# A decoder's three cross attentions: the order of work ahead of the first scores

## The reference

```python
x = x + _L1_xattn_ref(_layernorm(x), ctx_1024, ctx_1024, Wq, bq, Wk, bk, Wv, bv, Wo, bo)
# inside:
q = heads(layernorm(x) @ Wq + bq)          # 32 x 16 x 56 x 8
k = heads(ctx @ Wk + bk)                   # 32 x 16 x 1500 x 8
v = heads(ctx @ Wv + bv)
out = softmax(q @ k.T * scale) @ v         # per sequence and head
return merge(out) @ Wo + bo
```

## Time and profile before

| | |
|---|---|
| median of 3 runs | 3799.75 us (3795.43 to 3820.61) |
| profiled execution, its own time | 3812.16 us |
| its span in the trace | 3810.4 us |
| PE busy | 3447.9 us (90%) |
| DVE busy | 2381.6 us (63%) |
| ACT busy | 2087.9 us (55%) |
| POOL busy | 1618.1 us (42%) |
| mean granted share of PE's clock | 0.948 |

### The profile page before, as it was taken

How to read it: one execution, slowest core, us unless ns; L and a number is a source line. 1 busy time by engine, 2 the same in 40 slices (tenths; PEclk the granted TensorE clock), 3 DMA queues, 4 the chain that set the end, 5 groups by cost and what they waited for, 6 DMA issues and landing times. The chain is left out here.

```text
span 3810.4 us, 110666 instructions
## 1 busy us (share of the span) xinstructions
PE 3447.9 (90%) x46768; PEld 2411.7 (63%) x46768; DVE 2381.6 (63%) x4435; ACT 2087.9 (55%) x3581; POOL 1618.1 (42%) x1884
## 2 busy tenths in 40 slices
PE   7986669999999697889999999799999999999878
PEld 5654237777777344657777777343446777777548
DVE  5523568877776354468877776233667877777552
ACT  4333557777777222147777776334446777776511
POOL 1100157677674000047777664000336776776121
PEclk9999979999999798899999999899999999999967
DMA  4054136665664243036666564110015666656423
GB/s 164 2 227 168 47 84 155 153 159 144 154 156 97 51 117 82 4 88 152 149 160 148 149 158 100 47 61 23 13 43 140 156 154 152 159 145 153 123 68 106
DMA packets 206109, 439.22 MB, mean 115 GB/s; under 512 B 88210, under 2 KB 101111, under 8 KB 205448
## 3 DMA queue, kind: packets, MB, share of 16 engines
q1 hardware_dynamic: 202760, 430.07, 42.7%
q0 software_dynamic: 1440, 1.83, 0.2%
q10 hardware_dynamic: 1440, 0.52, 0.1%
HBM read 184.67 MB, written 5.40 MB: 50 GB/s over the span
## 5 line engine op out<-in xcount | busy, mean ns | idle before, releaser
L1562 DVE TENSOR_REDUCE x_bank_top<-ps 112x1 f32<-112x500 f32 x2304 | 1414.2, 672 | 447.8 <-PE ps L1264 440.8
L1410 ACT ACTIVATE x_probs_t<-ps 128x896 f32<-128x896 f32 x768 | 703.3, 916 | 127.6 <-PE ps L1285 122.6
L1264 PE MATMUL ps<-x_keys,x_queries 96*112 96x500 bf16 x2304 | 653.6, 382 | 42.5 <-DMA x_queries<-x_query_part 18.6
L1285 PEld LDWEIGHTS ps<-x_queries,x_keys 128*128 128x128 bf16 x9216 | 509.2, 97 | 245.6 <-issue 139.8
L1285 PE MATMUL ps<-x_queries,x_keys 128*128 128x112 bf16 x9216 | 580.9, 213 | 5.4 <-ACT x_probs_t L1410 4.2
L1299 PE MATMUL ps<-x_probs_t,x_values 128*32 128x112 f32 x18432 | 483.4, 261 | 8.9 <-ACT x_probs_t L1412 8.9
L1299 PEld LDWEIGHTS ps<-x_probs_t,x_values 128*32 128x32 f32 x18432 | 436.9, 110 | 70.1 <-issue 39.4
L1488 POOL TENSOR_TENSOR x_key_part<-x_key_whole,x_nothing 128x500 bf16<-128x500 f32 x270 | 337.3, 1249 | 256.8 <-ACT x_key_whole L1394 256.8
L1412 ACT ACTIVATE x_probs_t<-ps 128x448 f32<-128x448 f32 x768 | 414.5, 540 | 0.0
L1264 PEld LDWEIGHTS ps<-x_keys,x_queries 96*112 96x112 bf16 x2304 | 262.6, 131 | 170.9 <-DVE x_bank_top L1562 69.8
L1496 POOL TENSOR_TENSOR x_key_part<-x_key_left,x_nothing 128x500 bf16<-128x500 f32 x270 | 335.8, 1244 | 14.1
(11 more groups left out here) (510 smaller groups left out, 4332.1 us busy)
## 6 DMA issues: line engine op xcount, KB each, us to landing
x_keys<-x_key_part SPq DMA_DIRECT2D x1152, 192.0 KB, 3.8
x_ctx_t<-in_ctx_t SPq DMA_DIRECT2D x96, 750.0 KB, 6.2
cm_ctx_n<-in_ctx_n SPq DMA_DIRECT2D x32, 768.0 KB, 6.2
cm_ctx_t<-in_ctx_t SPq DMA_DIRECT2D x32, 750.0 KB, 8.6
x_queries<-x_query_part SPq DMA_DIRECT2D x558, 28.0 KB, 2.5
e_share<-m_weight_rows SPq DMA_DIRECT2D x32, 448.0 KB, 6.0
m_w<-in_L_ffn_experts SPq DMA_DIRECT2D x16, 768.0 KB, 5.7
e_share<-m_weight_rows SPq DMA_DIRECT2D x8, 896.0 KB, 5.3
```

Of the source, the lines that this page charges most:

```text
L1264: nc.tensor.matmul(ps[0:RW, n, 0:KB], queries[i // 2 % 2][0:TALL, p, i % 2, :], keys[i % 2][0:TALL, p, KB * n:KB * n + KB], start=True, st ...
L1285: mm = nc.tensor.matmul(ps[:, turned_bank(i, p) + c // VC, RW * (c % VC):RW * (c % VC) + RW], keys[i % 2][:, p, KT * c:KT * c + KT], queri ...
L1410: nc.scalar.activation(goal[:, 0:VR - 1], ps[:, bank:bank + VR - 1, 0:VC * RW], ACT.Exp, scale=scale).then_inc(exp_done, 1)
L1562: nc.vector.tensor_reduce(bank_top[0:RW, p, n:n + 1], ps[0:RW, n, 0:KB], AX_X, ALU.max).then_inc(topped, 1)
```

## The change

The same instructions are issued, three times as before, with other banks, in another order and with other waits:

- Norm takes the banks of the centred tokens as a list. Chunks 0 to 3 lie in banks 0, 3, 4, 5 and their means of squares in banks 1, 2, 1, 2. All pieces of the keys but the second go through bank 6.
- PE projects the three pieces of the keys of sequence 0 and the first chunk of the queries before it goes on with the norm of chunks 1 to 3. The last three pieces of the keys stand between the projections of the queries.
- ACT finishes chunk 0 of the norm, keeps and splits its queries and issues three slots of half 0; only then it takes the logarithm of chunk 1 and goes on. Its slots of half 1 come behind all that.
- SP waits for the high parts, issues three key slots, then slots of queries and keys by and by as their parts come.
- The scores of sequence 0 wait for the first kept chunk of the queries and the last logarithm instead of all four chunks; `scores_by_key` waits for all four.

```diff
-LEAD_BANKS = (6, 7, 6, 4, 5, 6)
+LEAD_BANKS = (6, 7, 6, 6, 6, 6)
+TOKEN_BANKS = (0, 3, 4, 5)
...
-        norm = Norm(chip, x, xn, True, scratch[:CH], scratch[CH:], (4, 5, 4, 5))
+        norm = Norm(chip, x, xn, True, scratch[:CH], scratch[CH:], (1, 2, 1, 2), None, TOKEN_BANKS)
...
             sp.wait_ge(zeros_ready, 2 * PARTS)
+            sp.wait_ge(lead_high, NB_)
+            for s in (0, 1, 2):
+                key_slots(sp, 0, 0, s)
+            sp.wait_ge(q_mid, 2)
+            query_slots(sp, 0, 0, 1)
+            query_slots(sp, 0, 0, 4)
+            sp.wait_ge(lead_mid, NB_)
+            key_slots(sp, 0, 0, 3)
+            key_slots(sp, 0, 0, 4)
+            sp.wait_ge(q_low, 2)
+            query_slots(sp, 0, 0, 2)
             sp.wait_ge(lead_low, NB_)
-            for s in range(SLOTS):
-                key_slots(sp, 0, 0, s)
-            sp.wait_ge(q_low, 2)
-            for h in range(2):
-                for s in range(SLOTS // 2):
-                    query_slots(sp, 0, h, s)
+            key_slots(sp, 0, 0, 5)
+            for s in (1, 4, 2):
+                query_slots(sp, 0, 1, s)
             stack_keys(0, 1)
...
                 if i == 0 and p == 0:
-                    pe.wait_ge(q_kept, CH)
+                    pe.wait_ge(q_kept, 1)
+                    norm.wait_log(pe, CH - 1)
...
             norm.centre(pe, 0)
-            norm.centre(pe, 1)
-            norm.power(pe, 0)
             pe.wait_ge(wk_landed, 2 * 16)
             lead_keys(0)
+            norm.power(pe, 0)
+            lead_keys(1)
+            lead_keys(2)
+            norm.centre(pe, 1)
+            pe.wait_ge(wq_landed, 3 * 16)
+            make_query(0)
+            norm.power(pe, 1)
             norm.centre(pe, 2)
-            norm.power(pe, 1)
-            lead_keys(1)
             norm.centre(pe, 3)
             norm.power(pe, 2)
             norm.power(pe, 3)
-            lead_keys(2)
-            pe.wait_ge(wq_landed, 3 * 16)
-            for c in range(CH):
-                norm.wait_scaled(pe, c)
-                nc.tensor.matmul(ps[:, c, 0:CT], wq[:], xn[:, CB * c:CB * c + CB, 0:S], start=True, stop=True).then_inc(q_made, 1)
-            for n in range(NB_, LEAD_KEYS * NB_):
-                lead_keys(n)
+            lead_keys(3)
+            make_query(1)
+            make_query(2)
+            lead_keys(4)
+            make_query(3)
+            lead_keys(5)
```

60 lines of the change are left out of this document (36 added, 24 removed).

## The result

The changed kernel is slower. In the first measurement its median was 3844.62 us (4 runs, 3821.36 to 3853.73) against 3797.59 for the kernel before (4 runs), a ratio of 1.010 with an interval of 1.0064 to 1.0135. Two later measurements of the same two kernels, 12 runs each of the changed one and 35 of the one before, gave 3829.46 against 3802.94 (1.0056, interval 1.002 to 1.0092) and 3830.54 against 3801.26 (1.0077, 1.0041 to 1.0112). The quotients of the medians, which take in every run, are 1.012, 1.007 and 1.008. One execution of the kernel before in the first of the two (3846.32 us) and three in the second (3848.48, 3853.39 and 11019.84) were slow ones, which the ratios leave out. By these two ratios the change costs 21 to 29 us.

What follows compares the result with a forecast made beforehand. DVE's row tops bound the pipeline, so the change only shifts its start: 6.0 + 4 + 5.5 = 15.5 us over three leads, 3799.75 + 15.5 = 3815 us. The range goes from 3797 to 3827.

Steps and rivals of the forecast that it cites:

- The chain from the squares to the first scores: First lead, from square of chunk 2 at 525.5 through PE and DVE to first scores at about 536.2.
- the shift of the first row tops: Start of the pipeline in three leads: row tops come later by 6.0 + 4 + 5.5 = 15.5 us.
- The clock's term: First lead: PE's clock falls at about 525 after 4.9 us idle, making work on the chain 2.35 us longer.
- The 4 and the 5.5: Shifts in us taken for the second lead, where the clock's fall moves against the chain, and for the third.
- "the same 3.5 to 4 us" for pair 1: First lead: row tops of pair 1 start at about 542 against 538.31, a shift like that of the first ones.
- rival (d): Second fall of the clock, over the first sequence's scores: 2 us more per lead, 3822 us; chance 0.10.
- The page's rule: DVE instructions with two SBUF inputs and GpSimd instructions reading SBUF exclude each other; without it, at most 1 us less per lead.
- the prediction's sentence about the slow rest parts: DVE's rest parts, 0.33 to 1.32 us for one shape, wait for POOL's instructions, which run without a break.
- (a): PE's clock doesn't fall in the leads, or falls where it costs nothing: 11 us, giving 3811; chance 0.20.
- (b): First scores start early because slots land 6 us earlier per lead: 18 us faster, giving 3782; chance 0.12.
- (c): Sequences 0 and 1 catch up the shift, since later keys are stacked earlier too: 3800 us; chance 0.13.

Runs made afterwards that it cites:

- the kernel whose clock was held: Changed kernel plus six spare subtractions of the mean on PE, unread, ahead of the means of squares of chunk 2: 3817.06 us, ratio 1.0052.

## Why the prediction was right and where it was wrong

**Right: what moves and what then comes last.** The first key slot at 9.1 us after the start (forecast 518.4 - 509.37 = 9.0), the last at 15.8 (15.6), and none of it used; the logarithm of chunk 1 behind ACT's slots at 13.6 (forecast 14.0 to 14.8); the first scores released by PE's own list; first row tops three microseconds behind the first scores (3.2; forecast 2.9). The experiments bear the mechanism out: taking ACT's slots away from the norm, or the splitting too, brings the row tops forward, and changing the order of PE's and DVE's turns doesn't. The chain from the squares to the first scores, which has these turns in it, was 10.7 us at the full clock in the forecast and is 11.2 from the start of L150 in the kernel whose clock was held.

**Near in size: the shift of the first row tops.** Forecast 15.5 us over three leads; measured 19.8, 15.7 and 16.8 in the three traces. By lead: 6.0 forecast and 7.2, 4.9, 4.5 measured; 4 and 5.1, 3.7, 5.1; 5.5 and 7.5, 7.2, 7.2. The clock's term, 2.35 us for lead 1, measured 3.5, 2.5 and 1.3. (Its sentence names the projection of chunk 1, but the sum prices only the means of squares and key piece 3.) The 4 and the 5.5 were taken and not added up from rows, so that the one for lead 2 lies among the measured values is luck; the one for lead 3 was too small in every trace, by 1.7 to 2.0 us.

**Wrong: "the same 3.5 to 4 us" for pair 1.** This is the step that failed. The shift was taken as finished with the first row tops: its growth from there on stood in the sum at nothing, although the same paragraph lists ACT's three slots ahead of keeping the first values. They cost as written: 1.85 us of issuing, and PE idle for 3.79 us until the second piece of the values. In the kernel before nothing of the sort stood there, since ACT had issued all six slots long before. The 3.95 us from pair 0 to pair 1 were 2.96 before, and in lead 1 a new gap stands ahead of pair 2, where the prediction let the row tops run on. The shift grows by 1.7 to 3.0 us over three leads until pair 1 and by 3.5 to 5.3 until pair 4 (the sums: 25.1, 19.2 and 20.8 there, against 19.8, 15.7 and 16.8). Without ACT's slots the growth is gone. The clock over the scores and values of pairs 1 and 2 is a part of it in some executions, the mechanism of rival (d), which I had given 0.10 and a price of 2 us per lead; it measured 0.8 to 2.1 together with the wait, and 1.2 in lead 1 where the clock was full. The price of (d), 22 us over the kernel before, is the one that came true; its mechanism is at most 0.8 of the 2.1 us in lead 1, and the rest is the wait for ACT, whose cause stood in my own sum.

**Not seen: the rest of the time.** At pair 4 the shift is 19 to 25 us, and the ratios of the two long measurements say 21 to 29. What is left is a few microseconds, and for those only this can be said: the runs of the changed kernel had a slightly lower mean clock (0.9479 and 0.9467 on average, those of before 0.9493 and 0.9504), which is 13 and 32 us more at 1.2 GHz and, at 0.47 us for each, an estimated 6 and 15 us. Part of that is the leads' own low stretches. Whether the new start also makes later stages lose their clock more often, or the rest is chance, stays open. The first median, 47 us above, rested on four runs; the one of them with a trace held the long low stretch shown above. What the other three held is not known.

**The page's rule.** The rest parts of the first queries took 2.48 us for two. POOL's timeline in that stretch:

```profile
515.30 1.14 POOL L1507 TENSOR_TENSOR x_key_part<-x_key_whole,x_key_part 128x500 bf16<-128x500 f32 x1
516.40 1.27 POOL L1505 TENSOR_TENSOR x_key_part<-x_key_whole,x_nothing 128x500 bf16<-128x500 f32 x1
```

This is on the prediction's sentence about the slow rest parts. POOL's two instructions end at 516.44 and 517.67, and DVE's pair ends at 517.80; ACT's middle parts start at 516.61 and 517.83, each about 0.16 us after one of POOL's ends. That is what the Trainium skill's page "SBUF — State Buffer", section "SBUF: two separate sides", says of a DVE instruction with two SBUF inputs beside GpSimd. The forecast had put it at no more than 1 us per lead. The kernel that splits behind the norm shows that this wait, with the work around it, was worth 1.8 to 3.5 us per lead, since the norm stood behind it; the wait alone was not taken out. In the second and third trace of the changed kernel ACT waited 0.74 and 0.28, and 0.75 and 0.23 us for these parts in lead 1, so it isn't the same in every execution either.

**The rivals.** (a), no fall of the clock, didn't happen in the first trace; in lead 2 of the second the chain took 11.3 us, as at the full clock. (b), an early start, didn't happen, and (c), a shift taken up later, didn't either: from pair 4 to the last row tops the three pipelines take 2056.1, 2054.1 and 2056.8 us, against 2051.1 and 2054.7 in two traces of the kernel before.

## What to carry to other kernels

When a step is brought forward on an engine that runs its list in order, write down what it now stands ahead of at every later place, too, and add the cost up to the point from which the bound engine has no gaps, not only to its first instruction. Here, stacking each part as soon as it is ready on an otherwise idle queue, with nothing else moved, made the three leads 6.3 us shorter to pair 4, and reordering three engines around it made them 19 to 25 us longer. Where one program's runs differ by 1% with the granted clock, four runs don't tell 15 us from 45: compare the traces stage by stage and repeat both kernels together.

## What the runs showed of the hardware that I hadn't expected

- The granted clock in one and the same program differs from execution to execution: 0.54 over 70 us of a stage in one and 0.95 in another, and the whole stretch took 509.7 and 484.3 us, 25 us apart.
- Issuing a slot of 28 KB costs ACT 0.62 to 0.74 us in the changed kernel and its variants (1.85 for three, 2.13 for three, 1.48 for two in the second trace) and 1.02 in the kernel before. That SP issues at the same time doesn't explain it by itself: in the changed kernel both issue two slots side by side, ACT from 517.84 us in 1.26 and SP from 518.14 in 1.20. Why the six of before are slower stays open. The Trainium skill's page "DMA: Bandwidth & Descriptors", section "Issuing engines are not separate DMA queues", says that several issuing engines save only the sequencer's time, "which is usually small relative to the DMA itself". Here that time was on the path: without any slot on ACT, the three leads are 9 to 15 us shorter to pair 4 (111.0 against 120.4 to 126.3), the clock's part in that included.
